# Key comparisons, zero stores, sums of squares and the first two products moved within a graph-and-attention layer

## What is computed

```python
xn = layernorm(x)
# graph part, twice: mean over the edges' sources, summed at their destinations
agg = segment_sum(h[src], dst);  mean = agg / max(deg, 1)
h1  = relu(xn @ W_self0 + mean0 @ W_neigh0 + b0)
gnn = h1 @ W_self1 + mean1 @ W_neigh1 + b1
# attention part
Q = elu(xn @ Wq + bq) + 1;  K = elu(xn @ Wk + bk) + 1;  V = xn @ Wv + bv
mix = gelu((Q * sum(K * V) / (Q * sum(K) + 1e-6)) @ Wo + bo)
x   = x + gnn + mix
x   = x + ffn(layernorm(x))          # 4-bit weights, 16-bit activations
```

## Time and profile before

| | us |
|---|---|
| median of three runs | 1296.41 |
| the profiled execution | 1292.26 |
| its span | 1290.4 |
| TensorE (matmuls) busy | 1165.9, 90% |
| TensorE weight loads busy | 630.2, 49% |
| VectorE busy | 685.1, 53% |
| GpSimd busy | 370.3, 29% |
| ScalarE busy | 353.5, 27% |

### The profile page before, as it was taken

How to read it: one execution, slowest core, us unless ns; L and a number is a source line. 1 busy time by engine, 2 the same in 40 slices (tenths; PEclk the granted TensorE clock), 3 DMA queues, 4 the chain that set the end, 5 groups by cost and what they waited for, 6 DMA issues and landing times.

```text
span 1290.4 us, 15376 instructions
## 1 busy us (share of the span) xinstructions
PE 1165.9 (90%) x6376; PEld 630.2 (49%) x6376; DVE 685.1 (53%) x1224; ACT 353.5 (27%) x440; POOL 370.3 (29%) x200
## 2 busy tenths in 40 slices
PE   3769999999999999981979999999999999959948
PEld 2435555555555544430434455444444445449924
DVE  6339568686366562302633443666564346653663
ACT  5433333233442433200241122222210012232530
POOL 1001567577768773787400000000000000000000
PEclk9889999999999999995999999999999999979979
DMA  8851653433442439114564033513221040000004
GB/s 237 347 190 50 166 144 73 133 62 59 87 103 18 107 80 335 11 1 113 186 254 175 20 107 108 165 52 99 88 76 50 17 163 1 1 1 1 1 23 137
DMA packets 140718, 130.33 MB, mean 101 GB/s; under 512 B 74892, under 2 KB 114060, under 8 KB 139624
## 3 DMA queue, kind: packets, MB, share of 16 engines
q1 hardware_dynamic: 73800, 128.78, 29.4%
q0 software_dynamic: 66560, 0.44, 5.2%
q10 hardware_dynamic: 288, 0.13, 0.0%
HBM read 101.25 MB, written 27.72 MB: 100 GB/s over the span
## 4 chain that ended last, share of the span: by engine, by line
PE 45%; DMA 17%; issue 14%; POOL 13%; DVE 5%; SPq 3%; ACT 2%; POOLq 0%; DVEq 0%; ACTq 0%
PE ps L988 20%; DMA at_scratch<-copies,cell 14%; POOL at_scratch L591 13%; PE ps L1050 7%; PE ps L1022 7%; PE ps L1072 6%; PE ps L1092 3%; DMA raw<-in_L_gnn_W_neigh_dram 2%; SPq L422 2%; SPq L471 1%; DMA parts<-at_scratch 1%; PE ps L1038 1%; DVE AT L1190 1%; PE ps L967 1%; DMA raw<-in_L_gnn_W_self_dram 1%
## 5 line engine op out<-in xcount | busy, mean ns | idle before, releaser
L923 PE MATMUL ps<-xnT,whl 128*128 128x512 f16 (+1 forms) x2304 | 410.9, 341 | 17.8 <-ACT Qs L752 15.5
L591 POOL DMA_INDIRECT at_scratch<-copies,cell x160 | 336.3, 2102 | 245.8 <-issue 165.0
L923 PEld LDWEIGHTS ps<-xnT,whl 128*128 128x128 f16 x2304 | 225.2, 98 | 201.0 <-issue 19.8
L988 PE MATMUL ps<-hb,hT 128*128 128x512 f16 x960 | 209.1, 379 | 1.3 <-DVE hT L1442 1.3
L988 PEld LDWEIGHTS ps<-hb,hT 128*128 128x128 f16 x960 | 93.5, 98 | 112.3 <-DVE hT L1442 1.8
L988 PE MATMUL ps<-hb,VT 128*128 128x512 f16 x480 | 105.6, 383 | 34.1 <-DVE x_acc L1394 32.6
L581 POOL PARTITION_ALL_REDUCE ag_fw<-am_fw x9 | 3.2, 353 | 370.4 <-DVE am_fw L1306 370.4
L988 PE MATMUL ps<-hb,xnT 128*128 128x512 f16 x480 | 106.5, 384 | 1.0 <-DVE hb L1293 1.0
L988 PEld LDWEIGHTS ps<-hb,VT 128*128 128x128 f16 x480 | 47.2, 99 | 92.0 <-DVE x_acc L1394 33.1
L1050 PE MATMUL ps<-P,AT 125*128 125x512 f16 x400 | 87.8, 379 | 0.0
L1022 PE MATMUL ps<-AT,P 125*128 125x512 f16 (+1 forms) x480 | 84.7, 339 | 0.0
(11 more groups left out here) (218 smaller groups left out, 1155.9 us busy)
## 6 DMA issues: line engine op xcount, KB each, us to landing
raw<-in_L_gnn_W_neigh_dram SPq DMA_DIRECT2D x32, 512.0 KB
parts<-at_scratch SPq DMA_DIRECT2D x20, 625.0 KB, 4.9
raw<-in_L_gnn_W_self_dram SPq DMA_DIRECT2D x24, 512.0 KB
at_scratch<-zeros SPq DMA_DIRECT2D x12, 1020.0 KB, 23.5
key_b<-key_scratch SPq DMA_DIRECT2D x8, 1250.0 KB, 9.5
raw<-in_L_mix_Wo_dram SPq DMA_DIRECT2D x16, 512.0 KB
x_all<-in_x_dram SPq DMA_DIRECT2D x9, 512.0 KB
x_acc<-in_x_dram SPq DMA_DIRECT2D x9, 512.0 KB, 9.4
```

The lines of the kernel that those rows point to most:

```text
L591: pool.indirect_dma_start(out=at_scr[c % 2][:, :], out_offset=bass.IndirectOffsetOnAxis(ap=cell[:, c:c + 1], axis=0), in_=copies[:, c:c + ...
L923: mm = pe.matmul(acc_of(c)[:, a:b], whl[:, i, wp, k, :], xnT[:, k, ap, a:b], start=(k == 0 and wp == 0 and ap == 0), stop=(k == KC - 1 and ...
L988: mm = pe.matmul(half_bank(i), stationary[:, k, ap, t * TP:t * TP + P], hb[:, n % 2, k, wp, :], start=(k == 0 and wp == 0 and ap == 0), st ...
```

## The change

Five moves; no arithmetic is added or removed.

- The zero stores leave SyncE's queue. GpSimd issues the same 12, once the zeros are set, the last tile of x and the fourth weight chunk have landed, and before its first indirect DMA.
- VectorE does `cells(0)` and `cells(1)` after the last `turned_lo`, ahead of `prepare_scale(1)`, and from then on two groups earlier than before: `cells(2g + 2)` and `cells(2g + 3)` in group g. The turned keys are copied there too. SyncE loads the keys for them at the head of its part of each group.
- ScalarE squares two of the next group's four chunks before it takes Q out of group 0, and the other two behind it; in the later groups all four come behind Q.
- Products 0 and 1 are issued by column group (`columns(c, n)`). A column group needs only the tiles of rows that it spans, so pieces of 12 matmuls stand between the turns 4 to 9.
- The transposes of the keys come before the last column group of product 0.

```diff
@@ SyncE
             load_keys(0)
             load_keys(1)
-            sp.wait_ge(zeros_set, 1)
-            for b in range(2):
-                for h in range(NZ):
-                    sp.dma_start(at_scr[b].rearrange("(h p c) o -> h p (c o)", h=NZ, p=P)[h],
-                                 zeros[:, :]).then_inc(zero_out[b], 16)
             load_ahead(4)
@@
             for g in range(KC):
-                load_ahead(6 if g == 0 else 5)
-                store_s(g)
                 for p in (2 * g + 2, 2 * g + 3):
                     if p < NPC:
                         load_keys(p)
+                load_ahead(6 if g == 0 else 5)
+                store_s(g)
@@ GpSimd, ahead of the indirect DMAs
+            pool.wait_ge(zeros_set, 1)
+            pool.wait_ge(x_in[NT - 1], 32)
+            landed(pool, at["chunk", 0, 3])
+            for b in range(2):
+                for h in range(NZ):
+                    pool.dma_start(at_scr[b].rearrange("(h p c) o -> h p (c o)", h=NZ, p=P)[h],
+                                   zeros[:, :]).then_inc(zero_out[b], 16)
@@ ScalarE
             chunk_hi(0, 3)
+            norms(2, (0, 1))
             for g in range(KC):
                 par = g % 2
-                if g + 1 < KC:
-                    norms(g + 2, range(4))
                 act.wait_ge(xn_done, 4 * g + 1)
...
                 act.activation(Qs[:, :], acc_of(4 * g)[:, 0:N], ACT.Identity,
                                bias=bias[:, BQ, g:g + 1], scale=inv[:, par, 0:1]).then_inc(xn_free[0], 1)
+                if g + 1 < KC:
+                    norms(g + 2, range(4) if g > 0 else (2, 3))
                 act.wait_ge(q_min, g + 1)
@@ TensorE
+            def columns(c, n, k0=0, k1=KC):
+
+                i = c % 4
+                a, b = NCOLS[n]
+                for k in range(k0, k1):
+                    for wp, ap in ((0, 0), (0, 1), (1, 0)):
+                        mm = pe.matmul(acc_of(c)[:, a:b], whl[:, i, wp, k, :], xnT[:, k, ap, a:b],
+                                       start=(k == 0 and wp == 0 and ap == 0), stop=(k == KC - 1 and wp == 1))
+                return mm
@@
             sums(0)
-            for t in range(4, NT):
-                turn_xn(t)
-            pe.wait_ge(xt_free, NT)
-            product(0)
-            sums(1)
-            product(1)
+            turn_xn(4)
+            pe.wait_ge(xt_free, 5)
+            worked(pe, at["chunk", 0, 0])
+            columns(0, 0, 0, 4)
+            turn_xn(5)
+            columns(0, 0, 4, KC)
+            turn_xn(6)
+            worked(pe, at["chunk", 0, 1])
+            columns(1, 0, 0, 4)
+            turn_xn(7)
+            columns(1, 0, 4, KC)
+            turn_xn(8)
+            pe.wait_ge(xt_free, 9)
+            columns(0, 1, 0, 4)
+            turn_xn(9)
+            columns(0, 1, 4, KC)
 
             pe.wait_ge(key_ok, 1)
+            pe.wait_ge(xt_free, NT - 1)
             for h in range(2):
                 mm = pe.transpose(bank(6)[:EP, h * EH:(h + 1) * EH], key_r[:, h, :], ident32[:EH, :EH])
             mm.then_inc(key_turned, 1)
+            pe.wait_ge(xt_free, NT)
+            columns(0, 2).then_inc(xn_done, 1)
+            columns(1, 1, 0, 4)
+            sums(1)
+            columns(1, 1, 4, KC)
+            columns(1, 2).then_inc(xn_done, 1)
@@ VectorE, after the last turned_lo
+            dve.wait_ge(key_turned, 1)
+            steps(dve.tensor_copy(key_c[:, :], bank(6)[:EP, 0:ET]))
+            cells(0)
+            cells(1)
             prepare_scale(1)
@@ VectorE, in group g
                 v_low(g)
-                if g == 0:
-                    dve.wait_ge(key_turned, 1)
-                    steps(dve.tensor_copy(key_c[:, :], bank(6)[:EP, 0:ET]))
-                if 2 * g < NPC:
-                    cells(2 * g)
-                    cells(2 * g + 1)
+                for p in (2 * g + 2, 2 * g + 3):
+                    if p < NPC:
+                        cells(p)
```

## The result

The changed kernel takes 1247.79 us (median of four runs, 1243.8 to 1251.47) against 1297.12 us before (with a fourth run of the kernel before); the ratio is 0.9612, with a 95% interval of 0.9571 to 0.9654. That is 49 us less, of 53 forecast. In later rounds the kernel before had medians of 1294.42 to 1294.85, so times in microseconds of different rounds compare to about 2 us; a ratio is taken against runs of the kernel before in the same round. The profiled execution of the kernel after is the slowest of the four, 1251.47 us, with a span of 1249.7 us.

The account below looks back on a forecast made before the run. The scatter's start and length, then 75.3 us, bound the time to the sum: 52.1 us earlier, plus 2.2 us of clock, makes 54.3, taken as 53. From 1292.3 that gives 1239, by the median 1243; range 1234 to 1258.

Parts of the forecast that it names:

- What bounds: Up to the sum at 674.43, the scatter's start plus its length, then 75.3 us from SyncE's release to the sum.
- Start of the scatter: First comparisons at 55.8, keys with 3 to 9 us of slack, first indirect DMA at 63: 59 us earlier.
- The zeros: Twelve stores from GpSimd, 2.3 us each to issue, hidden behind transfers lasting to 66, when the second column starts.
- Length of the scatter: GpSimd's indirect DMAs: last column starts at about 543 and lands at 547, 52 us earlier.
- The rival of a denser scatter: Columns cost 2.9 us under load, scatter ends by 540, TensorE's own work rules: 1240 us; chance 0.12.
- Products 0 to 6: TensorE's early products: product 2 at 75.6, 10.3 us earlier; the lead grows to 11.6 us at the first second product.
- The sum: After tile 29: the later of TensorE alone, 620.7, and the scatter, 622.3; 52.1 us earlier.
- TensorE cold between the turns: Every piece and turn runs at half clock: 17 us on the first comparisons, 13 on the end, 1256 us; chance 0.08.
- The rigid shift: After the sum TensorE runs on its own work, so moving that point moves the end by as much.
- Zeros throttled: GpSimd writes zeros in small descriptors, 400 us in all; scatter starts near 430, 1530 us at the extreme; chance 0.03.
- Scatter starts late: Keys stuck behind zeros, or slow GpSimd issue, put the first column at 70 to 80: 1249 to 1256 us; chance 0.2.
- Signs: First column 61 to 66, last 541 to 547, L1394 wait at most 3 us, SyncE unstuck, sum 620 to 625.

Follow-up runs that it names:

- scatter_140: The kernel after with the last 20 of 160 columns of edges left out of the scatter and SyncE's wait lowered to match; 1238.03 us.
- loads_first: The kernel after with SyncE loading the weight blocks due at a tile ahead of the piece of the counts and its wait; 1240.64 us.
- loads_first_cells1: The kernel after with weight blocks loaded ahead of pieces of the counts, and the second 20 columns compared behind the split of chunks 2 and 3; 1239.33 us.
- counts_later: The kernel after with the ten pieces of the counts moved three tiles back, the last ones a tile apart; 1254.49 us.
- keys_zeros_only: The kernel after without column groups between turns and with all four squares ahead of Q; keys and zeros stay moved; 1247.59 us.
- keys_delayed: The kernel after with the loads of keys 2 and 3 held until product 2 is done; 1245.15 us in one run.

## Why the prediction was right, point by point

- **What bounds.** Confirmed: in the kernel before, the kernel after and all nine variants whose sum waits, it follows SyncE's first pieces by 72 to 76 us (75.2 before; the 599.13 of the prediction stands in no row, and its 75.3 is 0.1 too much), whatever TensorE had gained early. In scatter_140 and loads_first TensorE's own work sets it; loads_first_cells1 has no wait at the sum either, but lost 4.4 us before it to the scatter's end.
- **Start of the scatter.** First column at 63.4, forecast 63; the first comparison at 56.16, forecast 55.8. The cost of the keys was no longer hidden, though: they had no slack, where I had 3 to 9 us, and the first comparison waited 0.2 us for them, which is one of the signs that I had named for a wrong prediction. Their store took 9.8 us beside the zeros (34.92 to 44.69), for which I had allowed 5; in the kernel before it took 1.7 (33.56 to 35.30).
- **The zeros.** The second column waits until 68.61, forecast 66. GpSimd issues the twelve in 6.64 us, 0.55 each; I had taken 2.3 from the indirect ones, and the real price lies below my lower bound of 1.36. It made no difference, since the transfers hid either.
- **Length of the scatter.** This is the mis-sized term. The last column starts at 552.9 instead of 543 and has landed by 556.6 instead of 547: 9.6 us late, which is the miss at tile 29 (631.8 against 622.3) but for 0.1 us. It has three parts of about the same size. First, my count doesn't add up: 19, 115.5, 6 and 18 columns are 158.5 and not 160, and 1.5 columns more are 3.5 us. Second, by 502 the scatter has started 139 columns, where I had 140.5. By 112 it has 15 and not 19, as 2.6 us go on the zeros and about 8 on the burst of keys 2 and 3, which I had called lighter loads; the long stretch to 466 has 116, as forecast, and the burst of loads to 502 has 8 where I had put 6. Third, the last 21 columns take 2.49 us each and not 2.33, 3.1 us in all. How much of this is chance can be seen from kernels with the same order of work up to about 500: the kernel after, counts_later and loads_first have done 131, 132 and 133 columns by 464.8, and start the last at 552.9, 550.4 and 549.4. The rival of a denser scatter is out.
- **Products 0 to 6.** Product 2 within 0.4 us; 10.4 us of idle, forecast 9.6. Product 4 waits 3.4 us for its chunk, forecast 2. Waits on Q in groups 1 to 3 are gone, as forecast; second products start 9.8 us earlier (466.63 against 476.43), forecast 11.6.
- **The sum.** 42.7 us earlier at tile 29 in the profiled executions, forecast 52.1. In the medians 49 against 53: the before's profiled execution was 4 to 5 us faster than its median, the after's 3.7 us slower, so the two medians lie closer to the forecast than the two profiles do, and that 49 comes as near to 53 as it does is in part luck of these executions. The wait of 4.8 us still let the clock fall (17.39 us against 15.6 for three tiles), where I had counted 2.2 us of gain. The rigid shift behind the sum held up to the last transposes ahead of the feed-forward products (1129.95 before, 1087.16 after, 42.8 us); 2 us of it are lost in the feed-forward part.
- **TensorE cold between the turns** didn't happen: five of six pieces take 2.75 us and their turns 1.02, at a granted clock of 1.00 from 36 on. But the argument from the row at 38.04, that transposes alone quicken, doesn't hold. In the kernel before, the next turns take 1.48 us (40.36) and 1.90 (42.58), and in keys_zeros_only, which has no pieces between them, the turns at 37.98, 40.30 and 42.52 take 1.90 to 1.93. What kept the clock up here were the pieces of matmuls between the turns. TensorE's timeline of the kernel before:

```profile
42.58 1.90 PE L897 MATMUL ps<-ident,xs 125*128 125x125 f32 x8 [0.73 <-DVE xnT L1162]
```

TensorE's timeline of keys_zeros_only:

```profile
40.30 1.93 PE L900 MATMUL ps<-ident,xs 125*128 125x125 f32 x8 [0.42 <-ACT xs L626]
```

The Trainium skill, "TensorE: Matmul & The Clock Gate", section "PE-mode transpose", says that the full clock doesn't engage for transposes. The turns without pieces bear that out for the most part; the turns of 1.02 us between pieces show that transposes do run at the full clock once it is up.

- **Zeros throttled** didn't happen: 383 GB/s on average between 26 and 66.
- **Scatter starts late**, rival 1, is half true in mechanism: the keys were late enough to touch the chain and cost 0.2 us.
- **Signs.** Those for the first column, L1394, product 2 and Q were met. The last column (552.9, not by 547), the sum (631.8, not by 625) and SyncE, which was still stuck until 59.3, missed.

## What to carry to other kernels

When the longest wait leads back to a serial chain on another engine, cost every early gain by what it does to the start and the density of that chain first: here two moves that filled TensorE's idle time brought nothing by themselves (ratio 1.0021), and moving 12 us of comparisons ahead brought about three quarters of the gain. Here the chain of small DMAs paid for a burst of large loads in both places where the burst was put. In a queue written out by hand, put loads that are ready ahead of those that must wait: swapping two statements took away the wait of 4.8 us that the order had caused. And compare ends of such a chain only beyond its own spread, 3.5 us here between kernels that are alike up to 500.

## What the runs showed of the hardware

- A store of 78 KB to memory took 9.8 us beside twelve 1 MB stores of another queue (after, 34.92 to 44.69), 1.7 us alone (before, issued at 33.56, with the loads behind it at 35.30).
- A plain 1 MB store costs GpSimd 0.55 us to issue (after, 6.64 us for 12), an indirect one of 125 elements 2.0 us (before and after, rows of the last column).
- Undisturbed, indirect DMAs follow each other every 2.3 us; over the stretch with the group loads every 3.0 to 3.1 us (91 to 92 GB/s); beside a pair of key loads of 2.5 MB GpSimd idled for 8.0 us (keys_delayed, 102.69), 8.9 us (after, 85.79, with two chunks) and 10.2 us (after, 190.53).
